# A graph layer on one core: one operand of layer 0's leaky step and scans, and of layer 1's scale product, read from PSUM

## The reference

```python
h = relu(layernorm(x))
# layer 0, per edge, softmax over the edges of one target, per feature
a = f_src[src] + f_dst[dst];  e = where(a >= 0, a, 0.2 * a)
ex = exp(e - segment_max(e, dst)[dst])
x = x + segment_sum(f_v[src] * ex / segment_sum(ex, dst)[dst], dst)
h = relu(layernorm(x))
# layer 1, per edge
scale = silu(silu(ea32 @ fc1 + b1) @ fc2 + b2) @ fc3 + b3
msg = silu(h[src] @ W_node * scale + ea16 @ W_sh)
alpha = softmax over all edges of a small network on (h[src], h[dst], ea32), mean of 8 heads
x = x + layernorm(h + segment_sum(msg * alpha, dst) @ W_out)
```

## Time and profile before

| | value |
|---|---|
| median of 3 runs | 3405.59 us |
| the profiled execution | 3394.61 us |
| its span | 3392.7 us |
| busy in the span: PE, DVE, POOL, ACT | 82%, 69%, 58%, 53% |
| layer 0's edges: first to last leaky step | 188.8 to 1489.0 us |
| granted TensorE clock, mean | 0.962 |

### The profile page before, as it was taken

The page is one execution under the profiler, slowest core; times in us unless marked ns, Lnnn a source line. Parts: engine busy times, 40 slices in busy tenths (PEclk is TensorE's granted clock), DMA queues, the critical chain, the costliest instruction groups (busy, mean ns, idle before and its releaser), DMA issues. The chain is left out here.

```text
span 3392.7 us, 83570 instructions
## 1 busy us (share of the span) xinstructions
PE 2774.3 (82%) x20718; PEld 2223.4 (66%) x20718; DVE 2354.0 (69%) x5011; ACT 1787.2 (53%) x3923; POOL 1966.7 (58%) x1957
## 2 busy tenths in 40 slices
PE   0678888887888888865599999999999999676764
PEld 0367777777877777753367766676666667455554
DVE  5598888888888888888255555555555555587876
ACT  6244444444444444435455555555555555566664
POOL 0077777777777777731577777777777777000001
PEclk9889999999999999987799999999999999799997
DMA  2576666666666666632688888888888888355552
GB/s 73 138 193 178 179 175 181 177 177 170 177 172 176 177 173 175 176 82 77 184 241 237 235 237 239 236 239 238 237 239 237 238 239 238 100 162 162 160 162 60
DMA packets 531315, 623.16 MB, mean 184 GB/s; under 512 B 83067, under 2 KB 410359, under 8 KB 531256
## 3 DMA queue, kind: packets, MB, share of 16 engines
q1 hardware_dynamic: 372038, 272.23, 29.2%
q0 software_dynamic: 89088, 243.39, 25.9%
q10 hardware_dynamic: 70130, 106.88, 9.8%
HBM read 534.78 MB, written 121.55 MB: 193 GB/s over the span
## 5 line engine op out<-in xcount | busy, mean ns | idle before, releaser
L866 POOL DMA_INDIRECT l_G<-rows_d,l_sidx x928 | 1005.4, 1083 | 298.7 <-issue 271.7
L1260 POOL DMA_INDIRECT l_G<-rows_d,l_sidx x928 | 911.2, 982 | 328.0 <-issue 250.0
L1390 ACT ACTIVATE l_h<-l_H,l_cols 128x512 f32<-128x512 f32 x464 | 317.8, 685 | 505.2 <-PE l_H L1297 492.1
L940 PE MATMUL l_accp<-l_ohe,H 128*128 128x128 f32 x3712 | 452.6, 275 | 0.0
L940 PEld LDWEIGHTS l_accp<-l_ohe,H 128*128 128x128 f32 x3712 | 433.6, 192 | 0.0
L1456 DVE TENSOR_TENSOR big<-l_SC,l_b 128x512 f32<-128x512 f32 x232 | 160.4, 691 | 354.0 <-PE l_SC L1326 353.7
L1619 PE MATMUL ag_accp<-ag_msg,ag_pick 128*128 128x128 f32 x1856 | 266.4, 289 | 139.7 <-DVE ag_pick L1661 130.2
L890 PE MATMUL l_A<-ident,l_G 128*128 128x128 f32 x928 | 149.1, 284 | 251.2 <-DMA l_G<-rows_d,l_sidx 210.9
L1619 PEld LDWEIGHTS ag_accp<-ag_msg,ag_pick 128*128 128x128 f32 x1856 | 227.1, 193 | 179.1 <-DVE big L1691 124.1
L1326 PEld LDWEIGHTS l_SC<-big,l_h 128*128 128x128 f32 x1856 | 238.9, 191 | 133.0 <-issue 133.0
L969 ACT ACTIVATE l_qe<-l_A 128x512 f32<-128x512 f32 x232 | 138.9, 599 | 351.5 <-PE l_A L895 344.1
(11 more groups left out here) (188 smaller groups left out, 5906.1 us busy)
## 6 DMA issues: line engine op xcount, KB each, us to landing
msg_d<-l_msg ACTq DMA_DIRECT2D x232, 256.0 KB, 2.7
ag_msg<-msg_d SPq DMA_DIRECT2D x232, 256.0 KB, 2.7
l_fd<-dst_d SPq DMA_DIRECT2D x464, 96.0 KB
l_pd<-dst_d SPq DMA_DIRECT2D x464, 96.0 KB
l_in<-ea_d SPq DMA_DIRECT2D x464, 80.0 KB
l_lo<-mark_d SPq DMA_DIRECT2D x464, 64.0 KB
l_G<-rows_d,l_sidx POOLq DMA_INDIRECT x1856
l_lo<-code_d SPq DMA_DIRECT2D x464, 64.0 KB
```

The costliest lines, as they stand in the source:

```text
L866: nc.gpsimd.indirect_dma_start(out=G[:, s, j, :], out_offset=None, in_=rows_d[0][:, :], in_offset=bass.IndirectOffsetOnAxis(ap=sidx[:, hal ...
L940: last = nc.tensor.matmul(accp[b][:, h, k, :], we_t[:, b, h * HJ + j, k * C:(k + 1) * C], oh_e[:, b, h * HJ + j, :], start=(j == 0), stop= ...
L1260: nc.gpsimd.indirect_dma_start(out=G[:, s, j, :], out_offset=None, in_=rows_d[1][:, :], in_offset=bass.IndirectOffsetOnAxis(ap=sidx[:, hal ...
L1390: nc.scalar.activation(out_t[:, s % 2, :], in_p[:, :], ACT.Silu, bias=cols[:, col:col + 1]).then_inc(ready, 1)
```

## The change

In layer 0, A is copied by ACT as before, but `leaky` now reads A in PSUM and its copy in SBUF, and writes A in place. `running` reads A and writes a new PSUM tile Q; `back` reads Q. ACT copies A a second time (`settle`, after `running`), since PE transposes e from SBUF. `link` copies Q's last column to a small tile, and now runs right behind `bring`, ahead of `settle`; `back` waits for `link` of its own item and not of the one before. The first column of `top_t` is made by a new one-column instruction (`ahead`). The codes are loaded by SP (two more DMAs per item) and `whose` is gone. PE's `front` waits for the second copy and for the scan, not for the first copy. In layer 1 the bias is added in place in SC, `message` reads it there, and `third` waits for the product that reads SC.

```diff
                 sp.dma_start(fd_t[:, s, h, :], dst_d[0][bass.ds(row[h], P), :]).then_inc(ld[s], 16)
+                sp.dma_start(code_t[:, s, h * HT:(h + 1) * HT],
+                             code_d[bass.ds(off[h], HT)].partition_broadcast(P)).then_inc(ld[s], 16)
 ...
             if after(i, 2):                                       # PE front
-                pe.wait_ge(a_copied, i - 1)
+                pe.wait_ge(e_copied, i - 1)
+                pe.wait_ge(q_ready, i - 1)
 ...
             last.then_inc(oh_ready, 1)                            # PE turn
+            pe.wait_ge(e_copied, i + 1)
 ...
-            nc.scalar.activation(who_t[:, s % 2, :], lo_t[:, s, 0:IT], ACT.Abs).then_inc(who_ready, 1)
 ...
+        def settle(lap, u, d):
+            act.wait_ge(q_ready, i + 1)
+            nc.scalar.activation(e_t[:, s % R, :], A[s % 2][:, :], ACT.Copy).then_inc(e_copied, 1)
 ...
             bring(lap, u, 2)                                      # ACT step
+            link(lap, u, 1)
+            settle(lap, u, 1)
             carry(lap, u, 0)
 ...
-            link(lap, u, 1)
-            whose(lap, u, 4)
 ...
-        for t, v in ((acc0, 0.0), (qe_t[:, :, :, :], 0.0), (lo_t[:, :, IT:IT + 2], -FAR)):
+        for t, v in ((acc0, 0.0), (last_t[:, :], 0.0), (lo_t[:, :, IT:IT + 2], -FAR)):
 ...
-            e = e_t[:, s % R, 1:IT + 1]
+            e = A[s % 2][:, :]
             dve.wait_ge(a_copied, i + 1)
-            nc.vector.scalar_tensor_tensor(out=e, in0=e, scalar=SLOPE, in1=e,
+            nc.vector.scalar_tensor_tensor(out=e, in0=e, scalar=SLOPE, in1=e_t[:, s % R, :],
                                            op0=ALU.mult, op1=ALU.max).then_inc(e_ready, 1)
 ...
-            nc.vector.tensor_tensor_scan(q_t[:, g, 1:IT + 1], lo_t[:, s, 0:IT], e_t[:, g, 1:IT + 1],
-                                         q_t[:, (g - 1) % R, IT:IT + 1], ALU.min, ALU.max).then_inc(q_ready, 1)
+            if after(i, 1):
+                dve.wait_ge(linked, i)
+                dve.wait_ge(top_ready, i)
+            nc.vector.tensor_tensor_scan(Q[:, :], lo_t[:, s, 0:IT], A[s % 2][:, :],
+                                         last_t[:, g:g + 1], ALU.min, ALU.max).then_inc(q_ready, 1)
 ...
-            if after(i, 1):
-                dve.wait_ge(linked, i)
+            dve.wait_ge(linked, i + 1)
 ...
-            nc.vector.tensor_tensor_scan(top_t[:, b, ::-1], lo_t[:, s, IT::-1], q_t[:, g, ::-1],
+            nc.vector.tensor_tensor_scan(top_t[:, b, IT:0:-1], lo_t[:, s, IT:0:-1], Q[:, ::-1],
 ...
+            nc.vector.scalar_tensor_tensor(out=top_t[:, b, 0:1], in0=lo_t[:, s, 0:1], scalar=top_t[:, b, 1:2],
+                                           in1=last_t[:, g:g + 1], op0=ALU.min,
+                                           op1=ALU.max).then_inc(ahead_ready, 1)
 ...
-                pe.wait_ge(scs, i - 1)                            # layer 1, third
+                pe.wait_ge(t_done, i - 1)
 ...
-            nc.vector.tensor_tensor(sc_t[:, s % 2, :, :], SC[s % 2][:, :, :],
+            nc.vector.tensor_tensor(SC[s % 2][:, :, :], SC[s % 2][:, :, :],
                                     b3_bc[:, :].unsqueeze(1).to_broadcast([P, TJ, C]), ALU.add).then_inc(scs, 1)
 ...
-            nc.vector.tensor_tensor(mine, G[:, s, :, 0:C], sc_t[:, s % 2, :, :], ALU.mult).then_inc(t_done, 1)
+            nc.vector.tensor_tensor(mine, G[:, s, :, 0:C], SC[s % 2][:, :, :], ALU.mult).then_inc(t_done, 1)
```

More of the change, by code:

```diff
@@ L797, in layer0_edges @@
                 lo_t = sb("l0_lo", [P, U, IT + 2], BF16, st)
-                who_t = sb("l0_who", [P, 2, IT], BF16, st)
+                code_t = sb("l0_code", [P, U, IT], BF16, st)
                 fd_t = sb("l0_fd", [P, U, 2, 3 * C], BF16, st)
                 oht = sb("l0_oht", [P, R, IT], BF16, st)
-                qe_t = sb("l0_qe", [P, R, 2, IT + 1], F32, st)
-                q_t, e_t = (qe_t[:, :, k, :] for k in range(2))
+                e_t = sb("l0_e", [P, R, IT], F32, st)
                 top_t = sb("l0_top", [P, 2, IT + 1], F32, st)
+                last_t = sb("l0_last", [P, R], F32, st)
                 front_t = sb("l0_front", [P, R], F32, st)
@@ L968, in bring @@
                                 act.wait_ge(wt_ready, i - R + 1)
-                            nc.scalar.activation(e_t[:, s % R, 1:IT + 1], A[s % 2][:, :], ACT.Copy).then_inc(a_copied, 1)
+                            nc.scalar.activation(e_t[:, s % R, :], A[s % 2][:, :], ACT.Copy).then_inc(a_copied, 1)
+                        def settle(lap, u, d):
+                            i, s, _ = item(lap, u, d)
+                            if not exists(i, NI):
+                                return
+                            act.wait_ge(q_ready, i + 1)
+                            nc.scalar.activation(e_t[:, s % R, :], A[s % 2][:, :], ACT.Copy).then_inc(e_copied, 1)
                         def link(lap, u, d):
@@ L1054, in onehot @@
                                 half = slice(h * HT, (h + 1) * HT)
-                                nc.vector.tensor_scalar(oht[:, g, half], who_t[:, s % 2, half], mine_bc[:, bass.ds(i * 2 + h, 1)], None,
+                                nc.vector.tensor_scalar(oht[:, g, half], code_t[:, s, half], mine_bc[:, bass.ds(i * 2 + h, 1)], None,
                                                         ALU.is_equal).then_inc(oht_ready, 1)
@@ L1084, in back, with ahead @@
                             dve.wait_ge(q_ready, i + 1)
-                            if after(i, 1):
-                                dve.wait_ge(linked, i)
+                            dve.wait_ge(linked, i + 1)
                             if after(i, 2):
                                 dve.wait_ge(wt_ready, i - 1)
+                            nc.vector.tensor_tensor_scan(top_t[:, b, IT:0:-1], lo_t[:, s, IT:0:-1], Q[:, ::-1],
+                                                         FAR, ALU.min, ALU.max).then_inc(top_ready, 1)
+                        def ahead(lap, u, d):
+                            i, s, lp = item(lap, u, d)
+                            if not exists(i, NI):
+                                return
+                            b = s % 2
+                            g, _ = ring(s, lp)
+                            dve.wait_ge(top_ready, i + 1)
+                            if after(i, 2):
                                 dve.wait_ge(front_ready, i - 1)
-                            nc.vector.tensor_tensor_scan(top_t[:, b, ::-1], lo_t[:, s, IT::-1], q_t[:, g, ::-1],
-                                                         FAR, ALU.min, ALU.max).then_inc(top_ready, 1)
+                            nc.vector.scalar_tensor_tensor(out=top_t[:, b, 0:1], in0=lo_t[:, s, 0:1], scalar=top_t[:, b, 1:2],
+                                                           in1=last_t[:, g:g + 1], op0=ALU.min,
+                                                           op1=ALU.max).then_inc(ahead_ready, 1)
                         def weigh(lap, u, d):
@@ L1138, in step @@
                             add(lap, u, -2, 1, at)
+                            ahead(lap, u, 1)
                             weigh(lap, u, 0)
```

26 lines of the change are left out of this document (12 added, 14 removed).

## The result

The changed kernel takes 3293.23 us (median of 4 runs, 3289.35 to 3297.24), beside 3408.28 for the one before (4 runs): a ratio of 0.966, interval 0.9641 to 0.968. The profiled execution took 3297.24 us, its span 3295.4.

The account below looks back on a forecast made before the run. POOL's gather issue was taken to bound layer 0. POOL at 5.24 and the loop at 5.21 us gave 5.30 an item from 5.63, 76 us, plus 3.4 for clearing: 3405.6 - 79 = 3326 us, range 3295 to 3385.

Parts of the forecast that it names:

- the sum: Layer 0: POOL 5.24 and loop 5.21 us lie close without slack, so 5.30 us an item was chosen.
- what is late next: Layer 0's loop through PE, ACT and DVE: 5.02 us, plus 0.14 for `weigh` later, plus 0.05 for PSUM: 5.21.
- The base: Layer 0's item in the kernel before, taken as 5.63 us from first and last starts over 231 items.
- POOL: Layer 0 gathers: mean falls from 1.091 to 0.97 us, `weigh` keeps 0.10 us an item, POOL's item becomes 5.24.
- PSUM as an operand: Layer 0 scans and leaky step reading PSUM: bounds 0 from L1456 against L1469, and 0.2 us each; 0.05 taken for `back`.
- `settle` and `link`: ACT in layer 0: `link`, `settle` and `carry` end before the transposes, so the second copy costs nothing, cover 0.1 us.
- More DMAs, ACT's freed time, layer 1: Two more SP transfers per item, `whose` gone from ACT, and layer 1 with PE full: each 0.
- The clearing: Before layer 0's first one-hot: 4104 columns of qe no longer cleared, minus 3.4 us.
- a scan holds POOL wherever its operands lie: Rival, layer 0: scans as such hold POOL, PSUM or not; 3379 to 3402 us, nearest no change; chance 0.07.
- The better case: Rival, layer 0: `weigh`'s part 0.05 and PSUM free, 5.16 to 5.19 us an item, 3298 us; chance 0.09.

Follow-up runs that it names:

- run with two gathers of four: Kernel before, and separately the changed kernel, issuing only two of four layer 0 gathers per item after the first 8 items: 3208.54 us, and 3249.69 us.
- three other kernels with all the holds of layer 0: Kernel before with layer 1's edit alone, 3406.27 us; with codes loaded by SP and ACT's marks pass gone, 3404.49 us; with indices copied one item early, 3390.78 us.
- kernel with early indices: Changed kernel, but POOL copies the next 8 items' indices one item early: 3251.66 us, ratio 0.9545.

## Why the prediction was wrong

The mechanism was right and so was the direction; the size was off. The step that failed is the sum: it took the loop, at 5.21 us, for as late as POOL, at 5.24, and so chose 5.30 us an item, from a base of 5.63. The runs showed a loop of 5.01, an item of 5.21, and a base of about 5.70.

*The loop (its "what is late next").* The prediction read 5.02 us from two starts of `front` in rows 6 and took it for the loop of the kernel before. Those five microseconds hold waits of their own: PE waits 0.28 and 0.39 us for the one-hots, and `weigh` starts 0.48 us behind the second `add` where 0.31 is the usual step, since it waits for ACT. In the run with two gathers of four they are there in the first ten items or so and then gone, and the loop is 4.81 us, DVE back to back. What the change adds is 5.01 - 4.81 = 0.20, where 0.14 + 0.05 stood, but that the numbers agree is partly luck: measured are 0.10 for `back` behind `link` (0.12 stood) and 0.13 for `ahead` (0.19), next to nothing for PSUM (0.05), 0.03 is gained elsewhere, and the 0.14 had the wait of `weigh` (0.17) taken off. So 5.21 should have been 5.01.

*The choice of 5.30 (its sum).* It rested on two bounds that lie close, 5.24 and 5.21, and put 0.06 on top. With the loop at 5.01 POOL bounds alone, and the item is POOL's own: 5.21 measured, 5.24 worked out. The 0.03 between these is a slip of the sum, which counts four pauses of 0.304 in every item and the copy's wait of 0.79 besides, though that wait stands in place of one pause in 32. The choice cost 231 x 0.09 = 21 us.

*The base.* 5.63 us came from one execution, with 1083 ns a gather, where three other kernels with all the holds of layer 0 show 1094 to 1098, and the two of them that differ in nothing else that counts 5.70 and 5.71 us an item. Those two ran a few us over their medians, so the kernel before is at 5.69 or 5.70 in its median. From 5.70 the same forecast gives 231 x 0.07 = 16 us more. The prediction had a sign of it: its POOL term went from 5.69 to 5.24, but its sum was taken from 5.63. The sum closes: 79 + 21 + 16 = 116, measured 115; to a few us this is chance, since the interval of the measured gain is 109 to 122 us. Put otherwise, the two profiled executions differ by 97 us, of which 1300.2 - 1203.1 = 97.1 are the loop of layer 0 and 3.1 its earlier start, less 2.9 lost behind it; the rest is that the first profile stood 13.7 us under its median and the second 4.0 over.

*POOL.* L870 was forecast at 0.97, measured 0.973, and the part that stays is `weigh`'s: 4 x (0.973 - 0.946) = 0.11 us an item, where 0.10 was taken.

*PSUM as an operand.* 0.05 us was allowed for `back`. Measured, in the median: the forward scan went from 1.285 to 1.289 us, the backward one from 1.218 to 1.220 (with one column less), the leaky step from 0.683 to 0.690. The bound from the nearest pair, 0, was right. The Trainium skill, "VectorE: DVE Perf Modes", section "The TRN2 errata", would add 62 cycles, an estimate of 0.065 us each; these rows show 0.002 to 0.007.

*`settle` and `link`.* Right that the second copy costs nothing behind the link; the experiment with the two exchanged shows how much hung on the order.

*More DMAs, ACT's freed time, layer 1.* 0, as forecast: one run shows it of the first two together, one of layer 1. The clearing: the first leaky step starts 3.1 us earlier where 3.4 were forecast. That is near the noise, as this start lies between 188.8 and 192.2 us in the profiles of the five kernels that clear and between 185.1 and 187.3 in the six that don't.

*The rivals.* That a scan holds POOL wherever its operands lie is refuted by the changed kernel and by the forward scan back on SBUF. The Trainium skill infers in "SBUF — State Buffer", "Who interferes with whom", that tensor_tensor does not stall descriptor generation. Here one does stall an indirect DMA: layer 1's gather went from 982 to 946 ns once the one tensor_tensor with two SBUF inputs had one in PSUM. But such a gather also reads its indices from SBUF (`l_sidx` in its row), and no run tells which part of it is held. So the runs show the gather held, and not that its descriptor generation is. The better case, given 0.09, was the one that came. Of its two conditions one held, PSUM costs nothing; the other, 0.05 for `weigh`'s part, did not (0.11), and the loop and the base made up the rest.

## What to carry to other kernels

Where GpSimd issues gathers one behind the other and bounds a stage, put one input of every long VectorE instruction into PSUM, as far as the copies and hand-overs this takes leave the rest of the loop shorter than the gathers: the instruction keeps its time and the gathers lose their stalls. Doing it for `weigh` too went too far here, 31 us slower. Before adding hand-overs for it, measure the loop behind the bound by taking half of the bounding work away; an interval read off a timeline may hold a wait. And look at what breaks the beat of the bounding engine: here a copy once in 32 gathers cost 42 us, where the wait for it was put at 14. And an idle time called "issue" can be a wait for another engine: look whether it always ends at the same distance behind that engine's instruction.

## What the runs showed of the hardware that was not expected

- A held gather ends 0.74 to 0.79 us behind the end of a scan and 0.81 to 0.85 behind the end of the leaky step, `weigh` or L1469 (230 gathers of the table).
- Only the beginning of a gather can be held. In the kernel with early indices `weigh` starts 0.11 us or more behind a gather's start, and the gather keeps its 0.95 us.
- A gather that starts right behind a holding instruction's start escapes, and how long this lasts depends on the instruction. In the kernel before those that start up to 0.10 us behind the forward scan's start take 0.95 us. Beside `weigh` they do so up to 0.04 us (one at 0.04 takes 1.47 already), and beside L1469 one at 0.03 takes 1.47. Why, no run shows. From the kernel with the forward scan back on SBUF:

```profile
900.07 1.30 DVE L1079 TENSOR_TENSOR_SCAN l_Q<-l_lo,l_last,l_e 128x512 f32<-128x512 bf16 x1
900.10 0.95 POOL L870 DMA_INDIRECT l_G<-rows_d,l_sidx  x1 [0.30 <-issue]
```

- The kernel before spreads over 23 us (3397.49 to 3420.9 in 19 runs), and the three others with all holds in layer 0 over 22 to 26 (10 runs each). The changed one, the one with early indices, the one with `weigh` from PSUM and the one with the second copy ahead of the link spread over 3 to 8 (4 or 5 runs each, and fewer runs spread less: four of the kernel before span 9). That fewer holding instructions make the time steadier was only argued.
